# Moving the first output product of each head group behind the attended values of the next step

## What is computed

```python
x = x + 0.5 * ffn(layernorm(x))
h = layernorm(x)
q, k = rope(h @ Wq.T), rope(h @ Wk.T);  v = h @ Wv.T     # 4 query heads share one k, v
dt = softplus(h @ Win.T + dt_bias);     g = dt * -exp(A_log_bias)
# for each head, chunk by chunk (G = cumsum of g inside the chunk):
scores  = q @ k.T                                        # 128 x 128
y_intra = (scores * causal_decay(G)) @ (v * dt)
y_inter = (q * exp(G)) @ state
state   = state * exp(G[-1]) + (k * exp(G[-1] - G)).T @ (v * dt)
y = rmsnorm(y_intra + y_inter) * gnorm_w * silu(h @ Wg.T)
x = x + y.reshape(L, H * D) @ Wo.T                       # the output product
x = x + 0.5 * ffn(layernorm(x))
```

## Time and profile before

| | us |
|---|---|
| median of 3 runs | 1642.57 |
| lowest and highest of them | 1641.81, 1643.51 |
| the profiled execution's own time | 1642.75 |
| its span (first to last instruction) | 1640.9 |
| PE busy in the span | 1589.4 |
| DVE, ACT, POOL busy | 1368.9, 1093.0, 1411.7 |

### The profile page before, as it was taken

How to read it: one execution, slowest core, us unless ns; L and a number is a source line. 1 busy time by engine, 2 the same in 40 slices (tenths; PEclk the granted TensorE clock), 3 DMA queues, 4 the chain that set the end, 5 groups by cost and what they waited for, 6 DMA issues and landing times.

```text
span 1640.9 us, 33589 instructions
## 1 busy us (share of the span) xinstructions
PE 1589.4 (97%) x11028; PEld 883.8 (54%) x11028; DVE 1368.9 (83%) x2945; ACT 1093.0 (67%) x2987; POOL 1411.7 (86%) x1316
## 2 busy tenths in 40 slices
PE   7898999999999999999999999999999999999986
PEld 5554555555555555555555555555555555555554
DVE  6988788888878888787878888788888878788876
ACT  4666677676766677766766667666776667666653
POOL 4767899888988899888998989888998889888974
PEclk8999999999999999999999999999999999999998
DMA  5123233232333223231332224323342224322222
GB/s 211 39 55 67 55 74 87 65 72 52 78 85 78 53 59 102 54 83 47 91 78 64 61 64 92 72 72 53 73 95 59 72 46 97 72 65 52 53 45 103
DMA packets 208012, 118.76 MB, mean 72 GB/s; under 512 B 173792, under 2 KB 174816, under 8 KB 206816
## 3 DMA queue, kind: packets, MB, share of 16 engines
q1 hardware_dynamic: 207840, 116.63, 29.7%
HBM read 70.19 MB, written 4.46 MB: 45 GB/s over the span
## 4 chain that ended last, share of the span: by engine, by line
PE 74%; POOL 11%; DVE 8%; issue 4%; ACT 2%; DMA 0%; ACTq 0%; POOLq 0%; DVEq 0%
PE B L325 23%; PE B L323 23%; PE B L324 23%; POOL QS L1410 2%; POOL ROWS L1423 2%; POOL RR L1456 1%; DVE WL L1696 1%; POOL PL L1445 1%; PE B L553 1%; POOL ZS L1449 1%; POOL WVF L1433 1%; POOL K L1417 1%; POOL WVL L1441 1%; POOL RM L1453 1%; DVE PF L1640 1%
## 5 line engine op out<-in xcount | busy, mean ns | idle before, releaser
L323 PE MATMUL B<-WH,XTH 128*128 128x128 bf16 (+1 forms) x992 | 269.3, 296 | 0.6 <-DVE QF L1610 0.6
L324 PE MATMUL B<-WL,XTH 128*128 128x128 bf16 (+1 forms) x992 | 269.3, 296 | 0.0
L325 PE MATMUL B<-WH,XTL 128*128 128x128 bf16 (+1 forms) x992 | 269.3, 296 | 0.0
L1410 POOL TENSOR_TENSOR QS<-QS,SIN 128x512 f32<-128x512 f32 x160 | 219.3, 1371 | 42.8 <-ACT QS L1137 42.7
L323 PE MATMUL B<-XTH,WH 128*128 128x512 bf16 x640 | 243.2, 380 | 1.0 <-DVE G L1630 1.0
L325 PE MATMUL B<-XTH,WL 128*128 128x512 bf16 x640 | 243.3, 380 | 0.0
L324 PE MATMUL B<-XTL,WH 128*128 128x512 bf16 x640 | 243.2, 380 | 0.0
L1689 DVE SCALAR_TENSOR_TENSOR YF<-B,RR,G 128x128 f32<-128x128 f32 x512 | 144.2, 344 | 113.4 <-POOL RR L1456 113.3
L1169 ACT ACTIVATE PF<-ROWS,NG 128x128 f32<-128x128 f32 x512 | 162.7, 389 | 79.1 <-POOL ROWS L1423 78.8
L1449 POOL TENSOR_TENSOR ZS<-YF,ZS 128x512 bf16<-128x512 f32 x128 | 158.0, 1235 | 64.5 <-ACT ZS L1207 64.2
L1136 ACT ACTIVATE QS<-B 64x512 f32<-64x512 f32 x160 | 94.9, 593 | 150.3 <-PE B L325 143.5
(11 more groups left out here) (209 smaller groups left out, 4320.9 us busy)
## 6 DMA issues: line engine op xcount, KB each, us to landing
ROWS<-rows_dram SPq DMA_DIRECT2D x128, 256.0 KB, 3.2
STAGE<-in_wall SPq DMA_DIRECT2D x108, 256.0 KB, 2.8
ACC<-in_x SPq DMA_DIRECT2D x3, 1024.0 KB, 10.0
out<-ACC SPq DMA_DIRECT2D x3, 1024.0 KB, 3.9
ZT<-ZS SPq DMA_TRANSPOSE x128, 3.1
ACC<-in_x SPq DMA_DIRECT2D x4, 256.0 KB, 3.6
COS<-in_cos SPq DMA_DIRECT2D x1, 1024.0 KB, 12.0
SIN<-in_sin SPq DMA_DIRECT2D x1, 1024.0 KB, 14.7
```

The costliest lines, as they stand in the source:

```text
L323: nc.tensor.matmul(out_, ah, bh, start=first, stop=False)
L324: nc.tensor.matmul(out_, ah, bl, start=False, stop=False)
L325: return nc.tensor.matmul(out_, al, bh, start=False, stop=last)
L1410: nc.gpsimd.tensor_tensor(QS[:, sl, :], QS[:, sl, :], SIN[:, t0:t0 + TB], ALU.mult).then_inc(sin_ready.sem, 1)
```

## The change

The output product of chunk 0 of each group leaves step 2, where it was the last thing on TensorE, and goes into step 3, directly behind `attend(3)` and ahead of slot B. Its addition on VectorE leaves the place behind `decayed(4)` and goes behind `state_lo(3)`. Nothing else is edited; the counts of instructions stay the same on all engines. The new lines move VectorE's line numbers by 2.

```diff
@@ tensor engine, step(g, n, last)
                 if s == 1 and n >= 2:
                     project_out(g, n - 2, last)
+                if n == PEEL:
+                    project_out(g, 0)
                 slot("B")
                 slot("C")
...
-                if s != 1 and n >= 2:
+                if s != 1 and n >= 2 and n % NCH != 2:
                     project_out(g, n - 2, last)
@@ vector engine, step(g, n, last)
-                if s != 2 and n >= PEEL:
+                if s != 2 and n > PEEL:
                     add_out(g, n - 3, last)
...
                 state_lo(g, n)
+                if n == PEEL:
+                    add_out(g, 0)
```

## The result

The changed kernel takes 1663.76 us (median of 4 runs, 1659.51 to 1664.28) against 1642.76 us before: ratio 1.0122, 95% interval 1.0105 to 1.0140. It is 21.0 us slower, where 19.7 us were forecast. The profiled execution is the shortest of the four, 1659.51 us with a span of 1657.7.

The account below looks back on a forecast made before the run. TensorE's program was taken to set the time (busy 1589.4 of 1640.9 us). Seven crossings at 2.45 us plus 2.6 in the first group make 19.75 us: 1642.6 + 19.7 = 1662.3 us, range 1651 to 1667.

Parts of the forecast that it names:

- the wait removed: Product of chunk 0 at each crossing into a new group: its wait for split weights goes, 1.51 us.
- scores(4): At a crossing, TensorE waits for POOL's low part of the last query head: new stall of 1.56 us.
- read_state(3): At a crossing, after the fill in slot A: the state's low part is ready just in time, at 332.57.
- attend(3): At a crossing, TensorE waits for gated(2), which ends at 333.92: a stall of 0.7 us.
- Its state part: State part of attend(3) at a crossing: waits for POOL's low part of the weighted values, 0.5 us.
- The addition: VectorE, behind state_lo(3): ends about 342.10, so the product of chunk 1 stalls 1.15 us at a crossing.
- the ready times of the side engines: Step 2 on ScalarE, VectorE and POOL: ready times hang on their own work and stay as traced.
- The queues: SyncE's queue behind turn_z(2): transpose lands at 341.8, weight pieces and rows start 1.6 us later; costed at nothing.
- First group: First group's crossing: product of chunk 1 starts at 152.5 instead of 149.89, 2.6 us later.
- Rival A: At scores(4): the stall goes and nothing takes its place, 18.5 us faster, 1624 us; chance 0.06.
- C: VectorE's step 3 gets ahead, addition not the last wait: 1.30 us a crossing, 1653 us; chance 0.09.
- D: TensorE's clock also falls at crossings: 0.5 to 1.65 us at each of seven, middle 1670; chance 0.07.

Follow-up runs that it names:

- e3: Against the kernel before: product of chunk 0 moved as in the change, its addition two places earlier, behind combine(3); 1655.05 us, ratio 1.0081.
- e1: Against the kernel before: only the product of chunk 0 moved behind attend(3), the addition left behind decayed(4); 1652.47 us, ratio 1.0064.
- e2: Against the kernel before: only the addition moved behind state_lo(3), the product left at the end of step 2; 1672.08 us, ratio 1.0170.
- e7: Against the changed kernel: VectorE's first pair of low-part splits replaced by one-column copies from the second group on; 1651.03 us, ratio 1.0065 to the kernel before.
- e5: Against the changed kernel: VectorE's first pair of low-part splits cut to 16 of 512 columns from the second group on; 1659.5 us.

## Why the prediction was right, and where it was off

*What bounds the kernel, and the wait removed.* Right. The wait went completely, and the kernel before without the pair of splits ran at a period of 186.24, 1.51 us below 187.75: the very number taken from the earlier trace rows.

*scores(4).* Forecast 1.56 us, measured 1.59. *read_state(3)* "just in time": 330.98 where 326.05 + 1.59 + 3.24 = 330.88, so 0.1 us. *attend(3)*: forecast 0.7, 0.43 on the row, 0.59 counted from the starts. *Its state part*: forecast 0.5, 0.44 on the row, 0.61 from the starts. *The addition*: forecast 1.15, 0.89 on the row, 1.05 from the starts. A row's idle time is shorter than the loss by about 0.16 us, since the matmul before is listed with 0.38 us where the next could start after 0.216. The sum of the starts is 1.59 + 0.1 + 0.59 + 0.61 + 1.05 - 1.51 = 2.43, against 2.45 forecast and 2.44 in the period. That the small errors of the five terms cancel is not luck: the last wait ends with the addition, so what an earlier term has too much, it has too little. Without the addition's term the same sum is 1.38, the 1.36 to 1.37 of e3 and e1.

*That the ready times of the side engines don't move with TensorE* held: state_lo(3) starts 13.00 us after the end of the fill in both kernels (339.05 - 326.05 and 340.79 - 327.79).

*The addition's part* was shown alone (2.43 of 2.44 us without moving a matmul), and so was the product's (1.37, forecast 1.30). They don't add: the addition's wait comes last and swallows what TensorE lost before it.

*The queues.* Costed at nothing, and nothing is seen of them: no wait of TensorE names the later transpose, and the stalls above account for the period without it. No run moves the product and leaves the queue as it was.

*First group.* Forecast 2.6. The anchor is attend(2), at 127.40 before and 123.42 after; the product of chunk 1 followed at 149.89 and 148.51. The distances are 22.49 and 25.09: 2.60 us more. The row, with its 1.98 us of idleness:

```profile
148.51 0.39 PE L323 MATMUL B<-WH,ZT 128*128 128x512 bf16 x1 [1.98 <-DVE ACC L1705]
```

That none of a delay is won back within the group, as the prediction has it for a crossing, does not hold here: read_state(4) starts at 156.77 before and at 155.01 now, so of the 2.60 us 2.22 are left; a short pause that the kernel before had ahead of its sums (L815, at 156.00) is gone.

*The sum* was 19.75 and the median moved by 21.0. The profiled run accounts for its own 16.8: -3.98 at the start (attend(2) came that much earlier, in work the change doesn't touch), 2.22, 17.1, and so 1.4 behind the last crossing, where the clock, 1.00 before the last steps, fell:

```profile
1593.00:1597.00 4.00, 2.43 (x24) 2.45 (x25) 2.97 (x10) 2.54 (x6) 2.91 (x3) 0.77 0.02 4
...
1597.00:1601.00 4.00, 3.78 (x20) 2.02 (x20) 2.62 (x7) 2.40 (x10) 2.31 (x3) 0.81 0.45 66
...
1601.00:1605.00 4.00, 4.00 (x39) 3.93 (x38) 2.01 (x6) 0.63 (x1) 3.84 (x7) 1.00 0.00 2
```

This was not foreseen. The start fits the 4.25 us by which the profiled run is below the median: the clock granted from 20 to 40 us was 0.88 in it and 0.77 in the kernel before, and from 95 to 110 us 1.00 and 0.89. The profiled runs of e2 and e7 started as early (attend(2) at 123.86 and 123.96) and are 9.6 and 5.5 us below their medians; the other kernels' profiled runs didn't. With the usual start the profiled run would have been 16.8 + 4.0 = 20.8 us slower than before, an estimate from these rows, and 21.0 were measured. So the extra 1.3 us of the median would be the late episode, if the unprofiled runs had it; that isn't seen. How much is lost behind the last crossing differs from kernel to kernel where their code is the same (1.0 us gained in e2, 5.7 lost in e3 and e5), so it isn't put down to the change.

*Rival A* (faster) and *C* (the addition not last) are out for this kernel; C is what e1 and e3 are. *D* (the clock falls at each crossing) did not happen in the profiled run of the changed kernel: the windows of 21 us over all seven crossings (from 324, 514, 704, 894, 1084, 1275 and 1465 us) stand at 1.00. It did at some crossings, at the price given for it (up to 1.65; 1.69 measured), in the addition alone, where the longest pause is 2.26 us and not 1.6.

## What to carry to other kernels

A wait on the busiest engine is worth removing only by the distance to the next thing that isn't ready: work that is moved away was also cover for the engines that follow, so read when each later input is ready before counting the wait as gained. If the work moved in its place is ready (here the next fill), the same step gains; if it is the late input itself, the step loses. And the consumer that frees a buffer has to be placed by the time its data are ready and its bank is wanted, not beside the instruction that was moved.

## What the hardware showed beside that

A pause of 2.2 to 2.3 us before a matmul was followed by TensorE's 1.2 GHz level at 5 of 7 crossings in one execution and 3 of 7 in another, at 1.69 us each as a rule, which is part of why the same program came out at 1662 or 1671 us. The pauses of 0.4 to 1.6 us of the changed kernel had no such effect at any of its seven crossings, nor had the one of 1.98 us in its first group (clock 1.00 from 142 to 320 us). The Trainium skill ("TensorE: Matmul & The Clock Gate", HAM oscillation) tells this of a loop whose pauses recur and are longer. The trace agrees in that each fall of the clock was paid for anew, with the addition that a pause of this length brings it only some of the time.

A VectorE instruction on 16 columns with two inputs in SBUF took as long as POOL's neighbours needed: 1.79 us for a pair. A pair of 512 columns took 1.47 us with POOL idle over most of it and 2.76 beside POOL's work. The Trainium skill ("SBUF — State Buffer", Who interferes with whom) says that a VectorE instruction with two SBUF inputs contends with a POOL instruction that reads SBUF, since its second input comes through the read interface that they share, and it calls the shared ports an exclusive lock. The trace agrees: the short pair went on only when POOL's two instructions had ended. It shows the use of it as well. A thirty-second of the columns saved 0.97 us of 2.76 here, while the full pair without POOL beside it is 1.29 us shorter; no run moved this pair away from POOL's work to see that gain.
